# Linear attention: scores and masks of batch zero between the second half's projections and maps, on other banks

## The reference, cut to what matters

```python
q, k, v = proj(wq), proj(wk), proj(wv)            # x @ w.T, split in 16 heads of 16
q = (q @ fq1_w.T + fq1_b) * (q @ fq2_w.T + fq2_b) # "maps": two products, biased, multiplied
k = (k @ fk1_w.T + fk1_b) * (k @ fk2_w.T + fk2_b)
...
s = jnp.where(mask, s, 0.0)                       # scores q.k, causal mask (chunks: plus running sum of k.v)
intra = jnp.einsum('bhncm,bhnmd->bhncd', s, vc)
o = (inter + intra)
o = o * jax.lax.rsqrt(jnp.mean(o * o, axis=-1, keepdims=True) + EPS) * norm_w
return o @ wo.T                                   # then x = layernorm(x + this)
```

## Time and profile before

| | us |
|---|---|
| median of 3 runs (1040.12 to 1041.12) | 1040.65 |
| the profiled execution, whole | 1037.62 |
| its span, first to last instruction | 1035.8 |
| TensorE busy in the span | 940.4 (91%) |
| VectorE busy | 695.1 (67%) |
| ScalarE busy | 461.2 (45%) |
| GpSimd busy | 373.9 (36%) |

### The profile page before, as it was taken

How to read it: one execution, slowest core, us unless ns; L and a number is a source line. 1 busy time by engine, 2 the same in 40 slices (tenths; PEclk the granted TensorE clock), 3 DMA queues, 4 the chain that set the end, 5 groups by cost and what they waited for, 6 DMA issues and landing times. The chain is left out here.

```text
span 1035.8 us, 18280 instructions
## 1 busy us (share of the span) xinstructions
PE 940.4 (91%) x7007; PEld 778.2 (75%) x7017; DVE 695.1 (67%) x1172; ACT 461.2 (45%) x1041; POOL 373.9 (36%) x364
## 2 busy tenths in 40 slices
PE   8788989988999999999999889999999778999970
PEld 5555656656888888888887568889889647999960
DVE  3466767876574655566554799768877575888846
ACT  4322435545545445644545344443323333666630
POOL 2000400003756666666673165554444123000005
PEclk9889969999999999999999999999999989999995
DMA  4000100004433433233331111040000128655513
GB/s 181 0 2 2 31 1 2 2 1 166 120 107 94 112 108 107 83 113 108 108 108 36 46 42 47 17 163 1 2 1 1 35 92 287 239 201 198 202 36 117
DMA packets 56885, 85.84 MB, mean 83 GB/s; under 512 B 4960, under 2 KB 47712, under 8 KB 54624
## 3 DMA queue, kind: packets, MB, share of 16 engines
q1 hardware_dynamic: 55264, 80.48, 24.2%
q0 software_dynamic: 1536, 4.20, 1.3%
HBM read 73.65 MB, written 11.01 MB: 82 GB/s over the span
## 5 line engine op out<-in xcount | busy, mean ns | idle before, releaser
L1640 ACT ACTIVATE e_probs<-ps,e_neg_max 128x256 f32<-128x256 f32 (+1 forms) x128 | 52.1, 419 | 125.3 <-DVE e_neg_max L1570 125.3
L1151 DVE TENSOR_TENSOR d_s_m<-ps,d_decay 128x768 f32<-128x768 f32 x64 | 58.3, 952 | 46.8 <-PE ps L1333 46.8
L123 PE MATMUL ps<-xTl,d_wh 128*128 128x512 f32 x192 | 79.5, 414 | 0.6 <-DVE xTl L577 0.5
L123 PE MATMUL ps<-xTh,d_wh 128*128 128x512 f32 x192 | 76.1, 396 | 0.0
L123 PE MATMUL ps<-xTh,d_wl 128*128 128x512 f32 x192 | 75.8, 395 | 0.0
L1246 ACT ACTIVATE d_gated_hi<-d_gated 128x512 fp32r<-128x512 f32 x32 | 20.2, 633 | 115.6 <-DVE d_gated L1157 115.6
L123 PE MATMUL ps<-wl_gated,f_wh 128*128 128x256 f32 x240 | 69.7, 290 | 2.1 <-issue 2.1
L1527 POOL TENSOR_TENSOR e_q_T<-xT 128x512 f32<-128x512 f32 x32 | 41.1, 1284 | 82.1 <-DVE xT L1558 82.1
L123 PE MATMUL ps<-wh_gated,f_wl 128*128 128x256 f32 x240 | 67.9, 283 | 0.0
L123 PE MATMUL ps<-wh_gated,f_wh 128*128 128x256 f32 x240 | 67.9, 283 | 0.0
L815 ACT ACTIVATE g_probs<-ps,g_neg_max 128x256 f32<-128x256 f32 (+1 forms) x128 | 43.2, 422 | 40.1 <-DVE g_neg_max L751 40.1
(11 more groups left out here) (368 smaller groups left out, 3069.3 us busy)
## 6 DMA issues: line engine op xcount, KB each, us to landing
f_stage<-in_w_experts SPq DMA_DIRECT2D x15, 1536.0 KB
d_decay<-in_decay SPq DMA_DIRECT2D x32, 384.0 KB, 3.7
d_stage<-in_w_decay SPq DMA_DIRECT2D x32, 256.0 KB, 3.2
d_stage<-in_w_decay SPq DMA_DIRECT2D x32, 128.5 KB, 3.5
d_stage_v<-in_w_decay SPq DMA_DIRECT2D x32, 128.0 KB, 2.3
d_stage<-in_w_decay SPq DMA_DIRECT2D x32, 128.0 KB, 2.5
slot_rows<-warm SPq DMA_DIRECT2D x1, 3840.0 KB, 13.2
slot_outs<-f_rows SPq DMA_DIRECT2D x15, 256.0 KB, 2.1
```

The costliest lines, as they stand in the source:

```text
L123: mm = pe.matmul(out, w(k), x(k), start=(n == 0), stop=(n == 3 * len(ks) - 1))
L1151: dve.tensor_tensor(s_m[:, s % 2, 2 * b:2 * b + 2, :], ps[:, 2 + 2 * b:4 + 2 * b, 0:CAUSAL], decay[:], ALU.mult).then_inc(sm_ready, 1)
L1640: ex = act.activation(probs[:, s % KEPT, i, cols], ps[:, 2 + i, cols], ACT.Exp, bias=neg_max[:, s % 4, t, i:i + 1], accum_out=sums[:, s % ...
```

## The change

`order` puts the two first V projections ahead of those of half 1. Projections 0 to 5 use banks 2 to 5 as before, 6 to 11 alternate between banks 6 and 7 and wait for the copy of the one two before. Maps 1 and 3 use banks 4 and 5 (map 1 therefore also waits for the copies of projections 2 and 3), all others banks 0 and 1; maps 5 to 7 wait for the factors of the map right before. TensorE makes `scores(0, i - 4)` behind `map_in(i)` for i = 4 to 7, with projection 4 + i behind them; the first scores wait for the factors of maps 0 to 3 and for six copies, and the wait for all factors moves to batch two. VectorE makes `masks(0, i - 4)` behind `factors(i)`, and splits the second half of x behind all weights. ScalarE takes the second factor of map i ahead of the copy of projection 4 + i for all i. `values` loses a wait on copies that the one for all 12 covers.

```diff
--- before.py
+++ after.py
@@ -173,15 +173,18 @@
         block = ctx.enter_context(nc.Block())
 
         Q, K, V = 0, 1, 2
-        order = [(Q, 0, 0), (Q, 0, 1), (K, 0, 0), (K, 0, 1), (Q, 1, 0), (Q, 1, 1), (K, 1, 0), (K, 1, 1), (V, 0, 0), (V, 0, 1), (V, 1, 0), (V, 1, 1)]
+        order = [(Q, 0, 0), (Q, 0, 1), (K, 0, 0), (K, 0, 1), (V, 0, 0), (V, 0, 1), (Q, 1, 0), (Q, 1, 1), (K, 1, 0), (K, 1, 1), (V, 1, 0), (V, 1, 1)]
 
         def bank_of(n):
-            return ps[:, 2 + n % 4, :]
+            return ps[:, 2 + n % 4 if n < 6 else 6 + n % 2, :]
 
         mapped = [(Q, 0, 0), (Q, 0, 1), (K, 0, 0), (K, 0, 1), (Q, 1, 0), (Q, 1, 1), (K, 1, 0), (K, 1, 1)]
 
         def map_banks(i):
-            return (0, 1) if i % 2 == 0 else (6, 7)
+            return (4, 5) if i in (1, 3) else (0, 1)
+
+        def map_freed(i):
+            return seconds(i) if i >= 5 else seconds(i - 1) if i >= 2 else 0
 
         def seconds(i):
             return sum(1 if kind == K else 2 for kind, _, _ in mapped[:i])
@@ -265,8 +268,7 @@
                 dve.tensor_copy(wh[:, n], w[:, n]).then_inc(w_hi, 1)
                 dve.wait_ge(w_hi, n + 1)
                 dve.tensor_tensor(wl[:, n], w[:, n], wh[:, n].bitcast(F32), ALU.subtract).then_inc(w_split, 1)
-                if n == 1:
-                    low(1)
+            low(1)
             dve.wait_ge(loaded, 16 * 5)
             for par in range(2):
                 dve.tensor_tensor(par_bias[:, par:par + 1], vecs[:, 1:2], c.parity[:, par:par + 1], ALU.mult).then_inc(bias_ready, 1)
@@ -274,14 +276,14 @@
             dve.tensor_copy(c.neg16[:], c.consts[:, C_NEG:C_NEG + CAUSAL])
             for i in range(len(mapped)):
                 factors(i)
-            for b in range(BATCH):
+                if i >= 4:
+                    masks(0, i - 4)
+            for b in range(1, BATCH):
                 masks(b, 0)
                 masks(b, 1)
-                if b >= 1:
-                    moments(b - 1)
+                moments(b - 1)
                 masks(b, 2)
-                if b >= 1:
-                    scale(b - 1)
+                scale(b - 1)
                 masks(b, 3)
                 if b >= 2:
                     add(b - 2)
@@ -340,12 +342,9 @@
             for n in range(4):
                 projected(n)
             act.wait_ge(bias_ready, 2)
-            for i in range(4):
+            for i in range(8):
                 second_factors(i)
                 projected(4 + i)
-            for i in range(4, 8):
-                projected(4 + i)
-                second_factors(i)
             for b in range(BATCH):
                 if b >= 1:
                     output(b - 1, 1)
@@ -366,7 +365,7 @@
                 kind, half, m = order[n]
                 pe.wait_ge(w_split, kind + 1)
                 pe.wait_ge(x_split, half + 1)
-                need(pe, p_ready, n - 3)
+                need(pe, p_ready, n - 1 if n >= 8 else n - 3 if n < 6 else 0)
                 if kind == V:
                     for t in range(2):
                         first = (4 * half + 2 * m + t) * P
@@ -382,7 +381,9 @@
             def map_in(i):
                 kind, half, m = mapped[i]
                 pe.wait_ge(p_ready, order.index(mapped[i]) + 1)
-                need(pe, f_ready, seconds(i - 1) if i >= 2 else 0)
+                need(pe, f_ready, map_freed(i))
+                if i == 1:
+                    pe.wait_ge(p_ready, 4)
                 tok = slice(half * 512, (half + 1) * 512)
                 for f in (1, 0):
                     mm = pe.matmul(ps[:, map_banks(i)[f], :], maps[:, 2 * kind + f, :], (q_all, k_all)[kind][:, m, tok], start=True, stop=True)
@@ -393,6 +394,9 @@
                 n = QUADS * b + quad
                 tok, late = slice(b * SEQ, (b + 1) * SEQ), slice(b * SEQ + P, (b + 1) * SEQ)
                 if n == 0:
+                    pe.wait_ge(f_ready, seconds(4))
+                    pe.wait_ge(p_ready, 6)
+                if n == QUADS * 2:
                     pe.wait_ge(f_ready, seconds(len(mapped)))
                 need(pe, sm_ready, 2 * n)
                 groups = [(ps[:, 2 + g, :], slice(ROWS * g, ROWS * (g + 1))) for g in range(4)]
@@ -405,7 +409,6 @@
             def values(b, quad):
                 par, m = quad // 2, quad % 2
                 n = QUADS * b + quad
-                pe.wait_ge(p_ready, 9 + b)
                 if quad == 0:
                     need(pe, on_ready, TPB * b)
                 if quad == 2:
@@ -448,26 +451,24 @@
             for n in range(4):
                 project(n)
             pe.wait_ge(loaded, 16 * 5)
-            for i in range(4):
+            for i in range(8):
                 map_in(i)
+                if i >= 4:
+                    scores(0, i - 4)
                 project(4 + i)
-            for i in range(4, 8):
-                project(4 + i)
-                map_in(i)
             pe.wait_ge(p_ready, 12)
             for b in range(BATCH):
-                scores(b, 0)
                 if b >= 1:
+                    scores(b, 0)
                     values(b - 1, 2)
                     values(b - 1, 3)
-                scores(b, 1)
-                if b >= 1:
+                    scores(b, 1)
                     turn(b - 1)
-                scores(b, 2)
+                    scores(b, 2)
                 if b >= 2:
                     project_out(b - 2)
-                scores(b, 3)
                 if b >= 1:
+                    scores(b, 3)
                     turn_back(b - 1)
                 values(b, 0)
                 values(b, 1)
```

## The result

| | before | after |
|---|---|---|
| median, us | 1040.88 (4 runs, 1040.12 to 1043.59) | 1030.46 (4 runs, 1029.25 to 1031.30) |
| ratio, 95% interval | | 0.9905 [0.9883, 0.9928] |
| span of the profiled execution | 1035.8 | 1029.5 |

Run twice more beside kernels before on the same chip, the change gave 0.9914 [0.9895, 0.9933] and 0.9913 [0.9893, 0.9933]. By the ratios it is 9 to 10 us faster; 1031.3 was forecast for the median. The two profiled executions differ by less, 1037.62 and 1031.30 us, where 1028.3 was forecast: the one of before lay 3.0 us under its median, the one after is 0.8 above. The parts behind the layer, further down, show where that comes from.

A forecast was written before the change was run, and what follows sets the result against it. Bound: TensorE and VectorE taking turns for 15.69 us. New scores 3.44, stalls 1.65 and values 1.32 make 6.41; 15.69 - 6.41 = 9.28; 1040.65 - 9.3 = 1031.3 us median (1028.3 profiled); range 1027.6 to 1034.8.

The forecast's parts named there:

- The half-idle stretch: From the last map to batch one's scores, first attention layer: 15.69 us of TensorE and VectorE taking turns, falling by 9.3.
- The walk: New order from map 0 at 14.61, instruction by instruction: batch one's scores start at 46.02 in place of 55.31.
- The stalls: TensorE waits before map 5, scores 1, map 6, scores 2 and values 0: 0.35, 0.11, 0.24, 0.11, 0.84, together 1.65 us.
- A switch of mode costs nothing: Eight switches between 32-row scores and 128-row products in the dense stretch: zero taken, upper bound 0.1 each, 0.8 us.
- The clock's share: Part of the 9.3 us due to the low clock of 45 to 55: 3.5 us at most.
- Tight banks: Maps 4 to 7 all use banks 0 and 1, so map i waits for the factors of map i-1.
- Rival B: Maps 4 to 7: masks lengthen the ring of banks, together 4 us; gain 5.3, 1035.3 us; chance 0.09.
- Rival A: Clock does not hold in the interleaved stretch, 28.8 to 46.0: +14 us there, kernel about 1045.4; chance 0.03.
- Rival D: The four masks only move the wait, values wait for a mask; the end stays at 1040.6 us; chance 0.03.
- Rival C: Later parts meet the clock's changes at another moment: 1.3 to 8.6 us more gain, 1022.7 to 1030.0; chance 0.12.
- the 1.5 that the prediction named as a sign against it: Stages behind the layer: one changing its length by over 1.5 us would show the forecast wrong.

The follow-up runs named there:

- the kernel before with halves: Kernel before, each set of scores made and handed over in two halves of two heads, nothing interleaved; ratio 0.9943 [0.9924, 0.9963] against before.
- the change with halves: The change, with every set of scores made and handed over in two halves of two heads; ratio 0.9879 [0.9855, 0.9903] against the kernel before.

## Why the prediction was right

It was right in sign, in place and in size: 9.3 us forecast, 8.8 in the layer (8.5 to 8.9 by the three profiles) and 8.9 to 9.9 by the three ratios. These are uncertain by 2 us each, so that the median came within 0.8 us of the forecast is in part luck. The profiled execution, forecast at 1028.3, took 1031.30: the prediction carried the 3.0 between before's profile and its median over to the kernel after, whose profile lies 0.8 above its median instead. By its steps:

- *The half-idle stretch bounds, and its loss is the layer's.* Shown: the layer's end moved by 8.83, batch one's start by 8.69.
- *The walk.* Map 5 at 31.42 forecast, 31.44 measured; scores 1 at 33.24 and 33.33; map 6 at 35.73 and 35.87; map 7 at 39.85 and 40.16; scores 3 at 41.56 and 41.97; values at 44.70 and 45.20; batch one at 46.02 and 46.62. The stalls are where they were put, and the error grows step by step to 0.6.
- *A switch of mode costs nothing.* This is the term that was mis-sized. I took zero from a mean at the low clock: 1.31 for a set of values is half of 2.62, but one more row parts it into 1.26 and 1.36 (52.69, 53.95, 55.31), and the second of these ends with the switch (the row stands below the list). The measured price is 0.10 in and 0.15 out. In the change: 1.80 from map 4 to scores 0 in place of 1.71, and from scores 0 to the second product of the projection (28.89 to 30.10) 1.21, where 0.86 and one product of 0.23 make 1.09. From map 4 to batch one the change took 19.53 us, where the walk has 18.91. By the starts of the rows the five stalls are 0.19, 0.09, 0.19, 0.08 and 0.85, together 1.40 in place of 1.65; so the switches took about 0.87, 0.22 a pair, and shorter waits for VectorE's results gave 0.25 of it back. With 0.1 for each switch the prediction itself had 8.5 for the layer, and 8.5 to 8.9 was measured.
- *The clock's share.* I gave 3.5 as an upper bound; 2.3 was measured. With the clock up the fourth mask becomes the late one (0.7), and scores 1 were slowed by 0.2 instead of 0.73, since the clock fell only while they ran.
- *Tight banks* cost 2.1 us when nothing fills them. My walk had their stalls right without saying that the scores would fill most of them. *Rival B*, a ring made longer by the masks, did not come: map 5 and map 6 waited 0.19 us each.
- *Rival A*: the clock stayed at 1.00 from 14.5 to 46.6. The prediction's ground against it, that it falls behind idle times of 1.94 us or more, does not hold by itself: in the kernel before with halves it fell at 44.2 behind idle times of 1.72 and 1.02, and with two of four scores moved it stayed at 1.00 behind one of 1.94 at 45.64. *Rival D*: only the copy of the last projection held the values, and taking that wait away gave 0.7 to 1.0. *Rival C*: the parts behind do change their length, by 3 us and once by more, in kernels with and without the change. In this pair of profiles the middle gave 0.8 and the experts' part took 3.3, which is over the 1.5 that the prediction named as a sign against it; the timed runs do not show such a loss.

The row of before that parts the two sets of values:

```profile
53.95 1.08 PE L417 MATMUL ps<-a_s_m,a_v_all 128*16 128x256 f32 x8
```

## What to carry to other kernels

Where two engines hand one set of banks back and forth, look for a dense stretch next to it that leaves the second engine idle, and walk the new order instruction by instruction: most of the gain here was the hand-over (6.3 of 8.7 us), the clock about a quarter. Freeing banks for such a move opens waits elsewhere, so price the banks alone; here their 2.1 us were mostly covered because the moved work lay in the same gaps. Count the switches between 32-row and 128-row products in a dense stretch at 0.24 us a pair.

## What the hardware showed that I had not expected

- A switch of tiling mode costs 0.10 us on the way in and 0.15 on the way out (1.94 us for 8 pairs), measured where TensorE is never idle; beside a gap it was not measured.
- Code that is the same in every kernel differs by about 3 us between profiles in two places, behind a 3.66 us gap (the clock's mean over 20 us 0.63 to 0.66 or 0.76 to 0.80) and at one weight transfer of the experts; a single profile can lie that far from its median.
- The longest idle time does not tell by itself whether the clock falls: it fell behind 1.72 and 1.02 us in one kernel and stayed up behind a single wait of 1.94 in another.
- Two heads at a time do not take half of four: a half of a set takes 0.54 us when it stands alone (49.71 to 50.25 in the change with halves) against 0.86 for the whole, so halves turn a batch of turns, in which neither engine was full (batch two of the change: TensorE 10.13 and VectorE 9.33 of 11.70 us), into one that TensorE bounds (10.95 of 11.06 us).
